# A bidirectional GRU over two image axes: VectorE's side work moved between two gates of a step

## The reference

```python
def step(h, xg):
    hg = h @ W_hh.T + b_hh
    xr, xz, xn = jnp.split(xg, 3, axis=-1)
    hr, hz, hn = jnp.split(hg, 3, axis=-1)
    r = jax.nn.sigmoid(xr + hr)
    z = jax.nn.sigmoid(xz + hz)
    n = jnp.tanh(xn + r * hn)
    h_new = (1.0 - z) * n + z * h
    return (h_new, h_new)
...
return (right + down + left + up) / 4.0
...
x = x + _L0_conv_ref(_gn(x), ...)
```

## Time and profile before

| | |
|---|---|
| time, median of 3 runs | 2526.6 us (2522.61 to 2531.65) |
| time of the profiled execution | 2523.95 us |
| its span, first to last instruction | 2522.2 us |
| TensorE busy | 2199.8 us (87%) |
| VectorE busy | 2035.9 us (81%) |
| ScalarE busy | 1621.5 us (64%) |
| GpSimd busy | 1533.2 us (61%) |
| granted TensorE clock, mean | 0.987 |

### The profile page before, as it was taken

The page is one execution under the profiler, slowest core; times in us unless marked ns, Lnnn a source line. Parts: engine busy times, 40 slices in busy tenths (PEclk is TensorE's granted clock), DMA queues, the critical chain, the costliest instruction groups (busy, mean ns, idle before and its releaser), DMA issues.

```text
span 2522.2 us, 80883 instructions
## 1 busy us (share of the span) xinstructions
PE 2199.8 (87%) x31528; PEld 1444.4 (57%) x31528; DVE 2035.9 (81%) x4883; ACT 1621.5 (64%) x3401; POOL 1533.2 (61%) x2114
## 2 busy tenths in 40 slices
PE   0679999899979999899979999899979999999995
PEld 0345555566546666566656666566656677555574
DVE  7229999777769999787879999888867777888874
ACT  0236666677758887676758788677657888666600
POOL 2016666667766666566766666667666677666610
PEclk9999999999999999999999999999999999999998
DMA  9983332347789997589999998589986655333699
GB/s 355 288 219 96 96 96 67 85 141 218 230 241 244 240 246 177 153 224 260 308 267 250 233 246 207 142 221 263 313 258 165 152 146 129 73 94 94 154 322 363
DMA packets 325723, 509.25 MB, mean 202 GB/s; under 512 B 24928, under 2 KB 140000, under 8 KB 325344
## 3 DMA queue, kind: packets, MB, share of 16 engines
q1 hardware_dynamic: 307296, 478.23, 69.0%
q10 hardware_dynamic: 18048, 25.85, 2.9%
HBM read 352.98 MB, written 151.01 MB: 200 GB/s over the span
## 4 chain that ended last, share of the span: by engine, by line
PE 34%; DVE 22%; ACT 22%; issue 11%; DMA 6%; POOL 3%; SPq 1%; ACTq 0%; POOLq 0%; DVEq 0%
PE bank L855 19%; DVE r L994 8%; ACT bank L663 8%; ACT r L655 7%; ACT z L659 7%; DVE h L1008 5%; DMA work<-x 4%; DVE bank L999 4%; PE bank L856 4%; PE bank L835 3%; DVE r L989 2%; PE bank L837 2%; PE bank L953 2%; POOL hsum L529 1%; DVE bn L1119 1%
## 5 line engine op out<-in xcount | busy, mean ns | idle before, releaser
L855 PE MATMUL bank<-h,wh 64*64 64x256 f32 x6144 | 1515.0, 384 | 121.2 <-DVE h L1008 120.6
L835 PE MATMUL bank<-seq,wx 64*64 64x256 f32 x6144 | 1551.3, 385 | 62.7 <-DMA seq<-seq_next 24.0
L837 PE MATMUL bank<-seq,wx 64*64 64x256 f32 x6144 | 1551.9, 385 | 0.0
L856 PE MATMUL bank<-h,wh 64*64 64x256 f32 x6144 | 1523.9, 386 | 0.3 <-issue 0.3
L537 POOL TENSOR_TENSOR v<-z,h 128x256 f32<-128x256 f32 x1024 | 746.9, 730 | 778.7 <-ACT z L659 777.6
L855 PEld LDWEIGHTS bank<-h,wh 64*64 64x64 f32 x6144 | 727.4, 132 | 483.6 <-PE bank L837 336.6
L835 PEld LDWEIGHTS bank<-seq,wx 64*64 64x64 f32 x6144 | 741.7, 132 | 355.9 <-DVE r L994 208.2
L545 POOL TENSOR_TENSOR hsum<-hsum,h 128x256 f32<-128x256 f32 x1024 | 752.0, 734 | 94.1 <-DVE h L1008 65.1
L837 PEld LDWEIGHTS bank<-seq,wx 64*64 64x64 f32 x6144 | 740.0, 132 | 16.7 <-issue 1.2
L856 PEld LDWEIGHTS bank<-h,wh 64*64 64x64 f32 x6144 | 730.3, 132 | 1.2 <-issue 0.7
L989 DVE SCALAR_TENSOR_TENSOR r<-bank,bhh,r 128x256 f32<-128x256 f32 x1024 | 491.0, 479 | 296.0 <-ACT r L655 242.3
(11 more groups left out here) (95 smaller groups left out, 2446.6 us busy)
## 6 DMA issues: line engine op xcount, KB each, us to landing
work<-x SPq DMA_DIRECT2D x384, 384.0 KB, 6.2
out<-work SPq DMA_DIRECT2D x192, 384.0 KB, 4.7
work<-x SPq DMA_DIRECT2D x143, 512.0 KB, 7.1
work<-x SPq DMA_DIRECT2D x286, 128.0 KB, 7.1
work<-x SPq DMA_DIRECT2D x32, 768.0 KB, 6.5
seq_next<-work SPq DMA_DIRECT2D x48, 512.0 KB, 6.3
work<-hsum_last SPq DMA_DIRECT2D x48, 512.0 KB, 6.5
seq<-x SPq DMA_DIRECT2D x17, 512.0 KB, 7.6
```

Source lines behind the costliest of these rows:

```text
L835: pe.matmul(as_pair(ps[LOW, :], c), wx[HIGH, gate, :], px[HIGH], start=start, stop=False, skip_group_check=True)
L837: return pe.matmul(as_pair(ps[HIGH, :], c), wx[LOW, gate, :], px[LOW], start=start, stop=False, skip_group_check=True)
L855: pe.matmul(ps[LOW, 0:N2], wh[LOW, gate, :], state[LOW], start=start, stop=True, skip_group_check=True)
L856: return pe.matmul(ps[HIGH, 0:N2], wh[HIGH, gate, :], state[HIGH], start=start, stop=True, skip_group_check=True)
```

## The change

The two half chunks of statistics move up: the first from behind h of the rows to between t2 of the rows and t1 of the columns, the second from the step's end to behind h of the rows. VectorE's output units are done in two halves of 256: the first where the whole was, at the step's end, the second in the next step between t2 of the rows and t1 of the columns. The waits for TensorE and for the load of x are in front of the first half, and `unit_finished` is set by the second.

```diff
-    assert len(unit_at) == UNITS and max(project_ends) < T and max(unit_at) + 1 < T and N_ACT % 3 == 0
+    assert len(unit_at) == UNITS and max(project_ends) < T and max(unit_at) + 2 < T and N_ACT % 3 == 0
...
-            def add_x(g, u):
-
-                k = TILES * (g - 1) + u // 3
+            def add_x(g, u, k):
+
+                tile = TILES * (g - 1) + u // 3
                 of = u % 3
-                dve.wait_ge(unit_ready, UNITS * (g - 1) + u + 1)
-                dve.wait_ge(xf_loaded[k % XFS], 32 * (k // XFS + 1))
-                to = xf[:, k % XFS, of, :]
-                dve.scalar_tensor_tensor(out=to, in0=unit_ps[:, :], scalar=unit_bias(u),
-                                         in1=to, op0=ALU.add, op1=ALU.add).then_inc(unit_finished, 1)
+                if k == 0:
+                    dve.wait_ge(unit_ready, UNITS * (g - 1) + u + 1)
+                    dve.wait_ge(xf_loaded[tile % XFS], 32 * (tile // XFS + 1))
+                px = slice(k * TILE // 2, (k + 1) * TILE // 2)
+                to = xf[:, tile % XFS, of, px]
+                ins = dve.scalar_tensor_tensor(out=to, in0=unit_ps[:, px], scalar=unit_bias(u), in1=to,
+                                               op0=ALU.add, op1=ALU.add)
+                if k == 1:
+                    ins.then_inc(unit_finished, 1)
...
                     make_t1(g, t, 0)
                     make_t2(g, t, 0)
+
+                    if stats:
+                        half_chunk_stats(g + 1, t, 0)
+                    if g > 0 and t - 1 in unit_at and unit_at[t - 1] >= N_ACT:
+                        add_x(g, unit_at[t - 1], 1)
                     make_t1(g, t, 1)
                     make_u(g, t, 0)
                     make_t2(g, t, 1)
                     make_h(g, t, 0)
                     if stats:
-                        half_chunk_stats(g + 1, t, 0)
+                        half_chunk_stats(g + 1, t, 1)
                     make_u(g, t, 1)
                     make_h(g, t, 1)
-                    if stats:
-                        half_chunk_stats(g + 1, t, 1)
                     if g > 0 and t in unit_at and unit_at[t] >= N_ACT:
-                        add_x(g, unit_at[t])
+                        add_x(g, unit_at[t], 0)
```

## The result

The changed kernel takes 2511.9 us (median of 11 runs) against 2524.2 of the kernel before (median of 11), a ratio of 0.9945 with a 95% interval of 0.9932 to 0.9958. By the ratio that is 14 us less, 11 to 17 by the interval; the two medians differ by 12. The forecast, 2506.5 us with 2498 to 2517, was on the right side and its gain of 18.2 us some 4 us too hopeful. How it comes to 14 is another matter: the steps gained somewhat more than the prediction said, and the starts of two sweeps and steps 103 and 120 of the same sweeps gave back about four times what it allowed for.

The account below looks back on a forecast made before the run. A loop through TensorE, VectorE and ScalarE bounds the kernel, none alone. Statistics 10.9 + units 7.8 + tails 3.1 - starts 3.6 = 18.2 us; from 2523.95 and 2526.6 that gives 2505.8 and 2508.4, forecast 2506.5, range 2498 to 2517.

Parts of the forecast that it names:

- What bounds a step: Plain step: r, t1 of the columns, u, t2, h0 end the loop; r allows t1 of the columns at 3.05.
- Statistics: Statistics steps of three sweeps: moved half chunks cut a step from 4.196 to 4.14 us, 10.6 us over 63 intervals each.
- Units: VectorE's split output units: each costs 0.03 and gains 0.11 us, 71 steps in the last three sweeps, 7.8 us.
- TensorE's tails: Unit steps before a long TensorE tail, two sweeps: the tail begins sooner, 22 x 0.14 = 3.1 us gained.
- What is later: Costs of moved work: starts of the second and third sweep lose 3.6 us; later unit ends and stores cost nothing.
- 1.8 later than now: Start of the second sweep, third alike: the first chunk's wait now precedes h0, 2 x 1.8 = 3.6 us lost.
- I cost this at nothing: SyncE's queue: stores wait 1.0 us longer, but loads of x go four steps ahead and land in 7.1; no cost.
- if SyncE's loads of x land after TensorE asks for them: Sign in SyncE's queue that would prove the prediction wrong: loads of x arriving after TensorE needs them.
- The other two signs: Statistics steps: prediction wrong if t1 of the columns starts later than 3.14, or u still follows the tanh at 3.52.
- Transfers take it: Rival, chance 0.08: DMA engines pace sweeps two and three, only first and last gain, 7.2 us, about 2517.
- Late stores make late loads: Rival, chance 0.03, slower: tiles stored 1.0 later delay loads of x in SyncE's queue, 22 us, 2528.
- No overlap on VectorE: Rival, chance 0.03, slower: each VectorE instruction behind another neighbour waits for the previous one's end, result 2560 us.

Follow-up runs that it names:

- The overfilled gap: Changed kernel with both half chunks between t2 of the rows and t1 of the columns, and the unit whole in the next step's gap: 2606.4 us, 1.0326.
- both cures: Changed kernel, first chunk's statistics in their old place in step 0, first two fetches three steps later: 2500.2 us, 0.9900; second run 2491.0 us, 0.9862.
- later fetches: SyncE's first two fetches of the next sequence three steps later: on the changed kernel 2499.3 us (0.9887), again 2502.8 (0.9901); on the kernel before 2517.1 (0.9971).
- The first-chunk experiments: Changed kernel with step 0's half chunks in their old places: 2505.0 us, 0.9911; with later fetches and the first chunk's load issued sooner instead: 2497.4 us, 0.9889.
- the one-step-later stores: Changed kernel with SyncE's stores of VectorE's tiles one step later in its queue: 2509.1 us, 0.9945.

## Why the prediction was right, and where its sizes were off

**What bounds a step** was read rightly: t1 of the columns behind ScalarE's r, then u, t2 and h0. The overfilled gap shows it, with 4.59 and 4.33 us against 4.60 and 4.32 worked out from the same rows.

**Statistics**: predicted 4.14 a step and 10.6 us for the three sweeps; measured 4.127, which is 4.28 us in the first sweep and would be 12.8 in all three. The term was 2 us too small because the rows' starts add up with roundings of 0.01 each and t1 of the columns leads to h0 in 1.05, not 1.06.

**Units**: 33 x 0.11 = 3.6 predicted for the last sweep, 3.83 measured. A half takes 0.40, the upper end of the bounds that were set.

**TensorE's tails**: 0.14 predicted for the step at 1073.88, 0.13 measured (4.87 to 4.74). For the second and third sweep, units and tails together should bring 7.3 us. With both cures they bring 3.8 + 3.8 = 7.6 (230.9 and 230.9 in the kernel before with later fetches, 227.2 and 227.1 in the second run of both cures), so the term was right. With the later fetches alone it is 1.9 + 3.5 (229.1 and 227.4), since step 109 of the second sweep takes 6.03 there instead of 4.11. In the changed kernel as it stands they bring next to nothing: 1.2 and 0.4 us longer in its first trace, 2.9 shorter and 1.0 longer in its second.

**What is later** is the part that failed, in two of its sentences.

"1.8 later than now" for a sweep's start was the reordering on VectorE alone, with plain steps behind it. Measured are 3.8. The rest is what the wait does to the other engines: TensorE's clock of 0.50 behind its idle time, 1.7 us in step 0, and GpSimd's late product, 0.9 in step 1 (the two make 2.5, from which 0.5 goes since the chunk came sooner). The first-chunk experiments take all of it away. The mechanism was right, the term was half its size: 7.6 us instead of 3.6.

"I cost this at nothing" for SyncE's queue looked at how late the stores are, and found 9 us of slack for loads that go out four steps ahead and land in 7.1. Neither holds at steps 103 and 120. At step 99 a fetch stands in front of the loads and waits 12.2 us for a store's landing, so the load for step 104 went out only 6.7 us ahead of h0 of step 103; and its last part, issued at 1165.20, took some 13 us to land. The kernel before had no slack left there, as its own 2.75 us wait of TensorE shows, and what the steps gain ahead of it comes back as waiting. The later fetches show it: 9 to 13 us on the changed kernel, 7 on the one before.

By its own words the prediction would be wrong "if SyncE's loads of x land after TensorE asks for them". They do, at step 103 of the second sweep and of the third. In the second sweep they did so in the kernel before as well, which the prediction did not look up. The other two signs stayed away: t1 of the columns at 3.08 and the tanh at 2.91. That the time still came out within 6 us of the forecast is in part luck: steps that gained 2 to 3 us more than forecast, and losses of 14 to 16 us in the traces where 3.6 were allowed, of which the time shows less.

Of the rivals, "Transfers take it" was half right: by the ratios, the waits at steps 103 and 120 took back 4 to 7 of 18 to 21 us. But it named the wrong limit, full DMA engines. They stay at 0.93 busy with the stall cured. "Late stores make late loads" is open: the one-step-later stores left the time the same, though that trace's stalls are shorter, and at step 120 store and load both go out over 1 us later. Later fetches cure step 120 with the units as late as before. "No overlap on VectorE" is refuted in both kernels, and with it the Trainium skill's rule (VectorE: DVE Perf Modes, The DRAIN you can't avoid) in its strict form: the next start comes 0.46 to 0.48 after that of a statistics instruction that lasts 0.55. The section itself adds that an instruction that is not held starts earlier.

The terms as measured in the traces are: about 13 us of statistics, 4 of the last sweep's units and 7.6 of units and tails in the middle sweeps, less 7 or 8 at the starts and 9 at steps 103 and 120 (6 or 7 in the second trace). That leaves 8 to 11 us, where the ratio says 14 (11 to 17). Some of the starts' loss is absorbed by later waits, and the rest of the difference stays open: single traces are uncertain by more than that, since the prologue alone differed by 4.3 us between the two traces, in code that the change does not touch, and step 70 by 3.2 (below).

## What to carry to other kernels

In a recurrence over several engines, look for the idle time in front of the instruction that decides the step, and fill it with side work by start-to-start distances, not durations; one piece more than it holds costs its full share. Before moving work that waits for a load, ask what the whole chain does in the one step where the load is late. And a queue that issues in order should have its waits for landings behind the loads that somebody needs soon; when the steps before such a wait get faster, more of it becomes visible.

## What the runs showed of the hardware

A single wait of 3 to 5 us ahead of the state was enough to halve TensorE's granted clock for the following 3 to 7 us at the starts, and again at step 103, where matmuls take 0.65 us at 1178.14 instead of 0.38 (there behind 4.05 us of idle time, in the kernel before behind 2.75). Through it and through GpSimd, moving one wait of VectorE cost 3.8 us where its place alone accounts for 1.8.

At step 70 of the first three sweeps the step takes either 4.4 or 7.6 us (5.9 in two cases), in any of the kernels, the one before too. The granted clock tells them apart. Step 70 of the second and the third sweep of the kernel before:

```profile
1036.09:1043.68 7.59, 0.83 (x2) 0.60 0.00 0
1610.94:1615.32 4.38, 0.83 (x2) 1.00 0.02 4
```

In the 14 traces the 27 short steps 70 all have a clock of 1.00, the 13 long ones 0.58 to 0.62, and the two of 5.9 have 0.80 and 0.81. Ahead of it, in step 69, VectorE's small instructions for the new weights keep TensorE waiting; whether its clock is down in step 70 or has already recovered differs from one execution to the next. Six of nine are long in the three traces with the statistics in their old places, seven of 33 in the other eleven. Whether the change has a part in that was not tested. It moves a single run by 3 to 10 us and is part of the spread of some 10 us that made the small ratios hard to tell.
